# Transposing DMAs on SyncE's queue, low halves at multiples of 16 bytes, and another buffer for the squares, in a four-layer graph kernel

## The chip, the cores and the metric

The kernel runs on one core of one Trainium2 chip. The time is the device time of one execution in microseconds, the median of several runs. The profile is of one further execution.

## The reference

Four graph layers work on x (4096 x 256) and one adjacency matrix adj (4096 x 4096), in float32. Each layer normalises its rows and applies a ReLU, and adds its result to x:

```
def ln_relu(x): return maximum((x - mean(x)) / sqrt(var(x) + 1e-5), 0)     # by rows
h = ln_relu(x);  A2 = adj + I;  s = diagonal(A2) ** -0.5
x = x + relu((s[:, None] * A2 * s[None, :]) @ (A2 @ h @ W0.T))
h = ln_relu(x) @ Wg;  hn = h / maximum(norm(h, rows), 1e-8)
x = x + softmax(hn @ hn.T + log(adj + 1e-8), rows) @ h + bias
h = ln_relu(x);  r = rowsum(adj) ** -0.5
x = x + relu((r[:, None] * adj * r[None, :]) @ h @ W2 + b2)
h = ln_relu(x)
for W in (W3a, W3b): h = relu(concat([h, adj @ h]) @ W)
x = x + h
```

## The kernel before

adj is passed six times (passes 0 to 5 in the code, `p`), each time for one product of the 4096 x 4096 matrix with 256 columns: passes 0 and 1 are the first layer's two products, pass 2 (`ATT`) is attention, pass 3 is the third layer, passes 4 (`TURNED`) and 5 are the last layer. A pass has eight groups `g` of 512 output rows, and a group eight chunks `c` of 512 input rows; a chunk is four blocks of 128. Products run in float16 with every float32 operand split into a high and a low half. The adjacency chunk is split by ScalarE (`ahi`, L771) and VectorE (`alo`, L1035) into one of two buffers; the 256 columns lie in `mov[0]` or `mov[1]` as rows of `MW = 2 * LO` elements per block: the high half, one more column (two are reserved, filled with ones, from F to LO), and the low half from LO on. With `LO = F + 2` the low half begins at byte 516 of a row of 1032 bytes.

TensorE's products per block and 128 output rows: in passes 1, 3 and 5 (`CROSS`) one matmul of 512 columns over both halves (L489) and one of 256 (L490); in passes 0 and 2 three matmuls, of 258 columns (L492), of the 256 of the low half (L493) and of 258 (L494); in pass 4 `mov` is the weights (L500 to L502). The sums of a group are read out by ScalarE (L808, cross terms into `o`) and VectorE (`add_cross`, L1043, which adds into `o`), and only then may TensorE write the bank again (`bank_free`).

A group's results go on during the next group. `PLACES` says after which chunk's split each engine does which step of the group before: "ev" (sums) after chunk 0, "h" (normalised rows, split into `hsp`; VectorE's half is L1149) after 4, "T" after 5, "W0" and "W1" (product of the rows with the layer's weights) after 6, in pass 1 "n0" and "n1" (rows divided by their norm, VectorE's half is L1187) and "G" after 7. `ATT_PLACES` says the same in blocks of attention. TensorE makes the small products of "W0W1" after part 1 of chunk 5 (L582 or L590 first), in attention after block 14 of the first group or 23 of the later ones. They need the rows turned by 128 x 128 blocks: "T" is a transposing DMA from `hsp` to `hT` (`turn_h`, L877), "G" one from `hsp` to `gnT` (`turn_gn`, L883), both issued by ScalarE's queue behind a wait for VectorE's half. There are 24 and 8 of them. ScalarE's groups of passes 1 and 3 are written out; those of passes 0, 4 and 5 are a loop. In pass 1 the squares of a row's values go to `junk` (L903) with their sum beside them; `o` is not in use between the split of the rows and the next group's sums.

SyncE's queue issues all other DMAs. In passes other than attention it is the load of 1 MB of adjacency per chunk (L330) into a ring of four; each waits until the chunk four before has been split (`split_ready`). In attention a step `H` is two blocks: it loads half a chunk (L380) once the numerators up to block 2(H - 3) are there, and, where the exponentials were made in an earlier group (the matrix of cosines is symmetric), a return of them from DRAM (L388), which TensorE turns (L669) three blocks ahead of their use; exponentials for later groups are sent out (L366). ScalarE makes `ahi` of the numerators (L974), VectorE the numerators (L1250) and `alo` (L1257).

```
def load(p, g, c, first=False):
    ...
    sp.wait_ge(split_ready, chunk_no(q, h, e) + 1)
PLACES = {0: ["ev"], 4: ["h"], 5: ["T"], 6: ["W0", "W1"], 7: ["n0", "n1", "G"]}
ATT_PLACES = [{2: ["ev"], 10: ["h"], 11: ["T"], 15: ["W0"], 16: ["W1"], 18: ["n0"], 19: ["n1"], 21: ["G"]},
              {2: ["ev"], 17: ["h"], 18: ["T"], 26: ["W0"], 27: ["W1"]}]
```

Of the kernel before, what the change touches and what calls it, by code (L numbers as in the profile page):

```python
# [41 lines left out]
F = 256  # L42
P = 128
NB = N // P
GB = 4
NG = NB // GB
NC = NB // GB
GR = GB * P
FB = F // P
LO = F + 2  # L50
MW = 2 * LO
LN_EPS = 1e-5
ADJ_EPS = 1e-8
# [3 lines left out]
W_SCALE = 64.0  # L57
# [11 lines left out]
ATT = 2  # L69
TURNED = 4  # L70


def build(nc, x, adj_t, w0, wg, bias_g, w2, bias_2, w3a, w3b, sent, out):
    f32, f16 = mybir.dt.float32, mybir.dt.float16
# [3 lines left out]
    with ctx:  # L78
        def sb(name, shape, dt):
            return ctx.enter_context(nc.sbuf_tensor(name, shape, dt))  # L80
# [4 lines left out]
        def sem(name):  # L85
            return ctx.enter_context(nc.semaphore(name))
# [29 lines left out]
        ev = sb("ev", [P, GB, F + 1], f32)  # L116
        o = sb("o", [P, GB, F], f32)
        oT = o[:, :, :].rearrange("p b n -> p (b n)").rearrange("p (f n) -> p f n", f=FB)
        hsp = sb("hsp", [P, GB, 2, F], f16)

        o2 = nums[:, 0:2, :].rearrange("p b n -> p (b n)").rearrange("p (b n) -> p b n", b=GB)
# [24 lines left out]
        ssq = sb("ssq", [P, GB], f32)  # L146
        ssqc = sb("ssqc", [P, GB], f32)
        rnorm = sb("rnorm", [P, GB], f32)
        junk = sb("junk", [P, GB, F], f16)


        acc = pb("acc", [P, GB, GR], f32)
# [45 lines left out]
        x_ready = sem("x_ready")  # L198
        stats_ready = sem("stats_ready")
        passed = sem("passed")  # L200
        mv_ready = sem("mv_ready")
        var_ready = sem("var_ready")
        rstd_ready = sem("rstd_ready")
# [30 lines left out]
        def at(passes, p, g, per=1, k=1):  # L234
            return (g + NG * passes.index(p)) * per + k
# [78 lines left out]
        def _(sp):  # L314
# [4 lines left out]
            def load(p, g, c, first=False):  # L319
                if not first:  # L320

                    q, h, e = (p, g, c - 4) if c >= 4 else ((p, g - 1, c + 4) if not isinstance(g, int) or g > 0
                                                            else (p - 1, NG - 1, c + 4))
                    if q == ATT:

                        sp.wait_ge(num_ready, h * NB + (GB * (c + 7) if c < 2 else GB * (c + 5)))
                    else:
                        sp.wait_ge(split_ready, chunk_no(q, h, e) + 1)
                row = g * (NC * P) + c * P
                sp.dma_start(ring[c % 4], adj_t[bass.ds(row, P), :]).then_inc(adj_loaded[c % 4], 16)  # L330
# [17 lines left out]
                sp.dma_start(bg[:, :], bias_g[0:1, :].to_broadcast([P, F])).then_inc(b_loaded, 16)  # L348
                sp.dma_start(b2[:, :], bias_2[0:1, :].to_broadcast([P, F])).then_inc(b_loaded, 16)

            def group(p, g, first=False):
                for c in range(2 if first else 0, NC):
                    load(p, g, c, first=first and c < 4)
                    if first and c == 3:
                        load_others()
                    if p == 5 and c == 5 and not isinstance(g, int):
                        store(g - 1)
# [41 lines left out]
            for p in range(6):  # L399
                if p == ATT:  # L400
                    for g in range(NG):
                        for H in range(NH):
                            before = (g, H - 4) if H >= 4 else (g - 1, H - 4 + NH)
                            if before[0] >= 0 and is_sent(*before):
                                send(*before)
                            att_half(g, H)
                else:
                    group(p, 0, first=p == 0)
                    with sp.Fori(1, NG) as g:
                        group(p, g)  # L410
# [68 lines left out]
        def _(pe):  # L479
            def product(p, g, c, b, k, first, last):  # L480


                jb = GB * c + k
                m = mov[p % 2]
                cols = slice(b * P, (b + 1) * P)
                hi, lo = ahi[:, c % 2, k, cols], alo[:, c % 2, k, cols]
                if p in CROSS:
                    both = m[:, jb, :].rearrange("p (s n) -> p s n", s=2)[:, :, 0:F]
                    nc.tensor.matmul(acc[:, b, :].rearrange("p (s n) -> p s n", s=2), hi, both, start=first, stop=False)  # L489
                    return nc.tensor.matmul(acc[:, b, 0:F], lo, m[:, jb, 0:F], start=False, stop=last)  # L490
                n = LO
                nc.tensor.matmul(acc[:, b, 0:n], hi, m[:, jb, 0:n], start=first, stop=False)  # L492
                nc.tensor.matmul(acc[:, b, 0:F], hi, m[:, jb, LO:LO + F], start=False, stop=False)  # L493
                return nc.tensor.matmul(acc[:, b, 0:n], lo, m[:, jb, 0:n], start=False, stop=last)  # L494
# [253 lines left out]
        def _(act):  # L748
# [117 lines left out]
                                     (psT2 if r == 1 else psT)[:, :, :, :].rearrange("p b q n -> p (b q) n"), ACT.Copy)\  # L866
                    .then_inc(hT_kept, 1)

            def turn_h(p, g):

                act.wait_ge(h_ready, at(SMALL, p, g))

                if not isinstance(g, int) or g > 0:
                    act.wait_ge(small_ready, at(SMALL, p, g - 1, 2, 2))
                else:
                    act.wait_ge(small_ready, at(SMALL, SMALL[SMALL.index(p) - 1], NG - 1, 2, 2))
                act.dma_start_transpose(hT[:, :, :], hsp[:, :, :, :].rearrange("p b s n -> p (b s n)"))\  # L877
                    .then_inc(hT_landed, 16)

            def turn_gn(g):  # L880

                act.wait_ge(gn_ready, at([1], 1, g, GB, GB))
                act.dma_start_transpose(gnT[:, bass.ds(g * GB * 2 * FB, GB * 2 * FB), :],  # L883
                                        hsp[:, :, :, :].rearrange("p b s n -> p (b s n)")).then_inc(gnT_landed, 16)

            def small_out(p, b):

                return small_bank(p, b)[:, -F:]

            def hi_of_small(p, g, r):  # L890
                act.wait_ge(small_ready, at(SMALL, p, g, 2, r + 1))
                if p == 3:
                    nc.scalar.activation(directT[:, bass.ds(g * FB, FB), 2 * P * r:2 * P * (r + 1)],
                                         (psW[:, :], psX)[r].rearrange("p (f n) -> p f n", f=FB), ACT.Copy,
                                         scale=1.0 / W_SCALE)\
                        .then_inc(direct_ready, 2)
                for b in (2 * r, 2 * r + 1):
                    if p == TURNED:
                        nc.scalar.activation(direct[:, blocks(g, b), :], small_bank(p, b)[:, 0:F], ACT.Copy, scale=1.0 / W_SCALE)\
                            .then_inc(direct_ready, 1)  # L900
                    if p == 1:

                        nc.scalar.activation(junk[:, b, :], small_out(p, b), ACT.Square, scale=1.0 / W_SCALE,  # L903
                                             accum_out=ssq[:, b:b + 1]).then_inc(ssq_ready, 1)
                    nc.scalar.activation(mov[(p + 1) % 2][:, blocks(g, b), 0:F], small_out(p, b), ACT.Copy,
                                         scale=dinv_w[:, blocks(g, b)] if p == 2 else 1.0 / W_SCALE)\
                        .then_inc(mov_hi, 1)
# [12 lines left out]
            def stage(name, p, g):  # L920

                if name == "ev":
                    evacuate(p, g)
                elif name == "h":
                    if p == 0:
                        hi_of_t(p, g)
                    elif p in SMALL:
                        hi_of_h(p, g)
                elif name == "T":
                    if p in TURN:  # L930
                        turn_h(p, g)
                elif p in SMALL and name in ("W0", "W1"):
                    hi_of_small(p, g, int(name[1]))
                elif p == 1 and name in ("n0", "n1"):
                    hi_of_gn(p, g, int(name[1]))
                elif p == 1 and name == "G":
                    turn_gn(g)


            PLACES = {0: ["ev"], 4: ["h"], 5: ["T"], 6: ["W0", "W1"], 7: ["n0", "n1", "G"]}  # L940
            ATT_PLACES = [{2: ["ev"], 10: ["h"], 11: ["T"], 15: ["W0"], 16: ["W1"], 18: ["n0"], 19: ["n1"], 21: ["G"]},
                          {2: ["ev"], 17: ["h"], 18: ["T"], 26: ["W0"], 27: ["W1"]}]

            def group(p, g, tp, tg):
                for c in range(NC):
# [57 lines left out]
            for p in range(6):  # L1003
                if p == ATT:

                    act.wait_ge(dinv_ready, 2 * NG)
                    for g in range(NG):
                        att_group(g, *((ATT, g - 1) if g else (1, NG - 1)))
                    hi_of_numerators(NG - 1, NB - 1)
                else:  # L1010
                    if p > 0:
                        group(p, 0, p - 1, NG - 1)
                    if p in TURN:

                        for g in range(1, NG):
                            group(p, g, p, g - 1)
                    else:
                        with act.Fori(1, NG) as g:
                            group(p, g, p, g - 1)
            stage("ev", 5, NG - 1)  # L1020


# [337 lines left out]
```

## Time and profile before

| what | value |
|---|---|
| median of 3 runs (lowest to highest) | 2461.54 us (2460.28 to 2462.68) |
| the profiled execution | 2456.39 us |
| its span, first to last instruction | 2454.6 us |
| TensorE busy (PE; weight loads PEld) | 2408.8 us, 98% (1614.4 us, 66%) |
| VectorE (DVE), ScalarE (ACT), GpSimd (POOL) busy | 1450.2, 1082.2, 143.7 us |
| mean granted TensorE clock | 0.996 |
| DMA | 490.00 MB, 200 GB/s |

The profiled execution lies 5.2 us below the median of the runs, 0.2%. Busy is an average over passes with different limits. A matmul's listed duration includes its way through the array, so matmuls that follow each other overlap; their pace is seen in the starts or in counts per time. An engine name with a q (ACTq) is its queue: issuing and waiting, while the engine itself is idle. PEclk or clock is the granted TensorE clock as a share of 2.4 GHz, 0.5 being 1.2 GHz. "DMA to landing" is from issue to the completion.

### The profile page before, as it was taken

Reading aid. Unit: us, or ns where it says so; the run is one execution under the profiler, and the core shown is the slowest. Engines: PE = TensorE matmul, PEld = TensorE weight load, DVE = VectorE, ACT = ScalarE, POOL = GpSimd, SP = SyncE. Lnnn points to the kernel's source line nnn. Section 1 sums busy time; section 2 is a strip of 40 time slices with the busy share of each in tenths; the row PEclk is TensorE's granted clock in tenths of the full one; section 3 lists DMA queues with packets and bytes.
Section 4 is the critical chain, followed back from the end, with each engine's and each line's share of the span. In section 5 each row is a group of like instructions: output and inputs, shape, how many; then the busy total and the mean of one; then the engine's idle time right before and its main releaser. Section 6 shows DMA issues by size and latency. Waiting matters only on the chain.

```text
span 2454.6 us, 41678 instructions
## 1 busy us (share of the span) xinstructions
PE 2408.8 (98%) x16584; PEld 1614.4 (66%) x16584; DVE 1450.2 (59%) x1907; ACT 1082.2 (44%) x1379; POOL 143.7 (6%) x114
## 2 busy tenths in 40 slices
PE   7999999999999999999999999999999999999999
PEld 7888887555556667777888666666544444566665
DVE  7645445675666566666777666566544454455555
ACT  6544444444444444444443444444444334443333
POOL 2300000111111000000000000001000000000000
PEclk9999999999999999999999999999999999999999
DMA  6455555656564866776778656555555445556553
GB/s 241 156 204 192 201 197 198 205 190 201 191 205 137 229 191 200 232 235 211 241 250 249 231 180 199 173 194 198 185 185 184 179 172 187 188 193 216 209 220 137
DMA packets 180289, 490.00 MB, mean 200 GB/s; under 512 B 80993, under 2 KB 114017, under 8 KB 139233
## 3 DMA queue, kind: packets, MB, share of 16 engines
q1 hardware_dynamic: 113344, 471.13, 55.5%
q10 hardware_dynamic: 66848, 17.57, 3.7%
q8 instruction: 63, 1.03, 0.2%
q14 instruction: 34, 0.27, 0.0%
HBM read 438.32 MB, written 33.55 MB: 192 GB/s over the span
## 4 chain that ended last, share of the span: by engine, by line
PE 90%; issue 3%; DVE 2%; ACT 2%; ACTq 1%; POOL 1%; DMA 1%; DVEq 0%; POOLq 0%
PE acc L489 25%; PE acc L490 12%; PE acc L493 8%; PE acc L492 8%; PE acc L494 8%; PE acc L502 5%; PE acc L500 5%; PE acc L501 5%; PE psS L683 2%; PE psS L685 2%; PE psS L684 2%; PE psS L669 2%; ACT ahi L771 1%; POOL rstd L432 1%; DMA hT<-hsp 1%
## 5 line engine op out<-in xcount | busy, mean ns | idle before, releaser
L489 PE MATMUL acc<-mov,ahi 128*128 128x512 f16 x3072 | 1004.2, 380 | 18.2 <-DVE o L1043 17.4
L490 PE MATMUL acc<-mov,alo 128*128 128x256 f16 x3072 | 839.5, 273 | 0.0
L1035 DVE SCALAR_TENSOR_TENSOR alo<-expo,ahi 128x2048 f16<-128x2048 f32 x160 | 366.6, 2291 | 348.4 <-ACT ahi L771 348.4
L492 PE MATMUL acc<-mov,ahi 128*128 128x258 f16 x2048 | 558.4, 273 | 4.8 <-DVE alo L1257 2.9
L493 PE MATMUL acc<-mov,ahi 128*128 128x256 f16 x2048 | 561.1, 274 | 0.0
L494 PE MATMUL acc<-mov,alo 128*128 128x258 f16 x2048 | 556.4, 272 | 0.0
L1035 DVE SCALAR_TENSOR_TENSOR alo<-adj,ahi 128x2048 f16<-128x2048 f32 x160 | 366.6, 2291 | 320.9 <-ACT ahi L771 318.8
L489 PEld LDWEIGHTS acc<-mov,ahi 128*128 128x128 f16 x3072 | 301.3, 98 | 383.6 <-DVE o L1043 19.8
L771 ACT ACTIVATE ahi<-expo 128x2048 f16<-128x2048 f32 x160 | 305.6, 1910 | 479.9 <-PE acc L490 297.5
L771 ACT ACTIVATE ahi<-adj 128x2048 f16<-128x2048 f32 x160 | 305.4, 1909 | 366.4 <-PE acc L490 178.4
L490 PEld LDWEIGHTS acc<-mov,alo 128*128 128x128 f16 x3072 | 301.3, 98 | 35.2
L492 PEld LDWEIGHTS acc<-mov,ahi 128*128 128x128 f16 x2048 | 196.9, 96 | 46.0 <-DVE alo L1257 5.6
L493 PEld LDWEIGHTS acc<-mov,ahi 128*128 128x128 f16 x2048 | 198.0, 97 | 39.5
L494 PEld LDWEIGHTS acc<-mov,alo 128*128 128x128 f16 x2048 | 202.1, 99 | 26.7
L974 ACT ACTIVATE ahi<-nums 128x512 f16<-128x512 f32 x256 | 160.0, 626 | 107.0 <-DVE nums L1250 102.0
L500 PE MATMUL acc<-ahi,mov 128*128 128x512 f16 x512 | 194.0, 379 | 0.0
L501 PE MATMUL acc<-alo,mov 128*128 128x512 f16 x512 | 194.0, 379 | 0.0
L502 PE MATMUL acc<-ahi,mov 128*128 128x512 f16 x512 | 194.0, 379 | 0.0
L1257 DVE SCALAR_TENSOR_TENSOR alo<-nums,ahi 128x512 f16<-128x512 f32 x256 | 175.2, 684 | 5.8 <-ACT ahi L974 5.7
L1250 DVE SCALAR_TENSOR_TENSOR nums<-adj,expo 128x512 f32<-128x512 f32 (+2 forms) x144 | 93.0, 646 | 131.3 <-ACT expo L957 130.8
L957 ACT ACTIVATE expo<-psS 128x512 f32<-128x512 f32 (+2 forms) x144 | 80.9, 562 | 201.9 <-PE psS L685 164.8
L432 POOL TENSOR_TENSOR rstd<-vare,neghalf 128x4 f32<-128x4 f32 x32 | 77.2, 2413 | 1160.2 <-DVE vare L1125 1160.2
(132 smaller groups left out, 2017.4 us busy)
## 6 DMA issues: line engine op xcount, KB each, us to landing
adj<-in_adj_t SPq DMA_DIRECT2D x160, 1024.0 KB, 4.8
expo<-in_adj_t SPq DMA_DIRECT2D x160, 1024.0 KB, 4.8
adj<-in_adj_t SPq DMA_DIRECT2D x128, 512.0 KB, 4.9
sent<-expo SPq DMA_DIRECT2D x112, 256.0 KB, 3.0
expo<-sent SPq DMA_DIRECT2D x56, 512.0 KB, 5.6
xres<-in_x SPq DMA_DIRECT2D x7, 512.0 KB, 10.0
out<-xres SPq DMA_DIRECT2D x7, 512.0 KB, 3.5
xres<-in_x ACTq DMA_DIRECT2D x1, 512.0 KB, 3.5
```

The costliest lines, as they stand in the source:

```text
L489: nc.tensor.matmul(acc[:, b, :].rearrange("p (s n) -> p s n", s=2), hi, both, start=first, stop=False)
L490: return nc.tensor.matmul(acc[:, b, 0:F], lo, m[:, jb, 0:F], start=False, stop=last)
L492: nc.tensor.matmul(acc[:, b, 0:n], hi, m[:, jb, 0:n], start=first, stop=False)
L493: nc.tensor.matmul(acc[:, b, 0:F], hi, m[:, jb, LO:LO + F], start=False, stop=False)
L494: return nc.tensor.matmul(acc[:, b, 0:n], lo, m[:, jb, 0:n], start=False, stop=last)
L500: nc.tensor.matmul(acc[:, f, :], hi, ahi[:, c % 2, k, :], start=first, stop=False)
L501: nc.tensor.matmul(acc[:, f, :], hi, alo[:, c % 2, k, :], start=False, stop=False)
L502: return nc.tensor.matmul(acc[:, f, :], lo, ahi[:, c % 2, k, :], start=False, stop=last)
L771: nc.scalar.activation(ahi[:, c % 2, :, :].rearrange("p b n -> p (b n)"), ring[c % 4], ACT.Copy, scale=ADJ_SCALE)\
L974: nc.scalar.activation(ahi[:, (j // GB) % 2, j % GB, :], nums[:, n % NUMS, :], ACT.Copy, scale=P_SCALE)\
L1035: nc.vector.scalar_tensor_tensor(alo[:, c % 2, :, :].rearrange("p b n -> p (b n)"), ring[c % 4], ADJ_SCALE, ahi[:, c % 2, :, :].rearrange( ...
L1257: nc.vector.scalar_tensor_tensor(alo[:, (j // GB) % 2, j % GB, :], nums[:, n % NUMS, :], P_SCALE, ahi[:, (j // GB) % 2, j % GB, :], ALU.mu ...
```

## The change

Both transposing DMAs move from ScalarE's queue to SyncE's, each behind its waits, which sit on a `sem_inc` of a new semaphore. In passes 1 and 3 the rows' one goes behind the load of chunk 0 and the normalised rows' one behind the load of chunk 3 of the group two later; in attention behind steps given by H. SyncE's first two groups of these passes and the first two of pass 4 are written out, and ScalarE's groups become a loop in every pass but attention. LO becomes F + 8: the low half begins at byte 528, and a row has 1056 bytes. The three-matmul form keeps its 258 columns. The squares go to `o`'s bytes, and `junk` is gone.

```
-LO = F + 2
+LO = F + 8
+        squares = o[:, :, :].rearrange("p b n -> p (b n)").bitcast(f16).rearrange("p (b n) -> p b n", b=2 * GB)
-        junk = sb("junk", [P, GB, F], f16)
+        turning = sem("turning")
@@ SyncE
-            def group(p, g, first=False):
+            def turn_h(p, g):
+                sp.wait_ge(h_ready, at(SMALL, p, g))
+                sp.wait_ge(small_ready, at(SMALL, p, g - 1, 2, 2))
+                sp.sem_inc(turning, 1)
+                sp.dma_start_transpose(hT[:, :, :], hsp[:, :, :, :].rearrange("p b s n -> p (b s n)"))\
+                    .then_inc(hT_landed, 16)
+            def turn_gn(g):
+                sp.wait_ge(gn_ready, at([1], 1, g, GB, GB))
+                sp.sem_inc(turning, 1)
+                sp.dma_start_transpose(gnT[:, bass.ds(g * GB * 2 * FB, GB * 2 * FB), :],
+                                       hsp[:, :, :, :].rearrange("p b s n -> p (b s n)")).then_inc(gnT_landed, 16)
+            def group(p, g, first=False, turned_rows=None):
                 for c in range(2 if first else 0, NC):
                     load(p, g, c, first=first and c < 4)
+                    if turned_rows is not None and c == 0:
+                        turn_h(*turned_rows)
+                    if turned_rows is not None and turned_rows[0] == 1 and c == 3:
+                        turn_gn(turned_rows[1])
...
                             att_half(g, H)
+                            if g == 0 and H == 1:
+                                turn_h(1, NG - 2)
+                            elif g == 0 and H == 3:
+                                turn_gn(NG - 2)
+                            elif g == 0 and H == 8:
+                                turn_h(1, NG - 1)
+                            elif g == 0 and H == 12:
+                                turn_gn(NG - 1)
+                            elif g > 0 and H == 11:
+                                turn_h(ATT, g - 1)
+                elif p in (1, 3):
+                    group(p, 0)
+                    group(p, 1, turned_rows=(ATT, NG - 1) if p == 3 else None)
+                    with sp.Fori(2, NG) as g:
+                        group(p, g, turned_rows=(p, g - 2))
+                elif p == TURNED:
+                    group(p, 0, turned_rows=(3, NG - 2))
+                    group(p, 1, turned_rows=(3, NG - 1))
+                    with sp.Fori(2, NG) as g:
+                        group(p, g)
@@ TensorE
-                n = LO
+                n = F + 2
@@ ScalarE: turn_h and turn_gn, which were there, are gone, and "T" and "G" from stage, PLACES and ATT_PLACES
-                        nc.scalar.activation(junk[:, b, :], small_out(p, b), ACT.Square, scale=1.0 / W_SCALE,
+                        nc.scalar.activation(squares[:, b, :], small_out(p, b), ACT.Square, scale=1.0 / W_SCALE,
-                    if p in TURN:
-                        for g in range(1, NG):
-                            group(p, g, p, g - 1)
-                    else:
-                        with act.Fori(1, NG) as g:
-                            group(p, g, p, g - 1)
+                    with act.Fori(1, NG) as g:
+                        group(p, g, p, g - 1)
```

## Rows read from the trace of the kernel before

**Rows 1.** Windows, passes 0, 4, 5: busy PE, PEld, DVE, ACT, POOL; clock, DMA.

```profile
200.00:380.00 180.00, 180.00 (x1632) 157.88 (x1631) 91.48 (x77) 76.63 (x67) 13.56 (x9) 1.00 0.55 198
...
1800.00:2080.00 280.00, 280.00 (x1299) 126.90 (x1298) 135.48 (x97) 112.61 (x108) 0.00 (x0) 1.00 0.50 180
2180.00:2420.00 240.00, 240.00 (x1479) 144.57 (x1478) 127.59 (x82) 96.24 (x71) 0.00 (x0) 1.00 0.59 212
```

**Rows 2.** Waits of TensorE: total us, times, longest us.

```profile
PE acc L489 <- DVE o L1043: 17.4, 6, 4.3
...
PE acc L492 <- DVE alo L1257: 2.9, 2, 2.2
PE psW L582 <- DMA hT<-hsp: 2.3, 1, 2.3
PE psW L590 <- DMA hT<-hsp: 1.9, 1, 1.9
```

**Rows 3.** Windows of 10 us over gaps in pass 1, attention and pass 3.

```profile
478.00:488.00 10.00, 5.79 (x27) 2.84 (x25) 7.88 (x11) 4.80 (x6) 0.00 (x0) 0.83 0.52 148
525.00:535.00 10.00, 8.40 (x53) 4.89 (x51) 7.21 (x8) 4.91 (x6) 0.00 (x0) 1.00 0.80 243
...
1329.00:1339.00 10.00, 7.83 (x56) 6.43 (x55) 5.07 (x9) 3.04 (x5) 0.00 (x0) 0.83 1.08 234
1435.00:1445.00 10.00, 7.74 (x53) 5.79 (x52) 2.92 (x3) 1.78 (x4) 0.00 (x0) 0.83 0.55 198
```

**Rows 4.** Chain that ended last, 466 to 484 us: start us, us, what.

```profile
473.98 3.95 ACTq L883
...
478.03 1.92 ACT ahi L771
...
482.66 0.39 PE acc L489
```

**Rows 5.** Timeline of VectorE, 470 to 486 us: start us, us, engine, line.

```profile
479.97 2.29 DVE L1035 SCALAR_TENSOR_TENSOR alo<-adj,ahi 128x2048 f16<-128x2048 f32 x1 [6.03 <-ACT ahi L771]
482.18 1.41 DVE L1043 SCALAR_TENSOR_TENSOR o<-acc,o 128x256 f32<-128x256 f32 x4
```

**Rows 6.** Timelines of SyncE, ScalarE and TensorE around 455 to 463 us.

```profile
454.36 5.52 SPq L330 DMA_DIRECT2D adj<-in_adj_t  x2
...
455.32 4.33 ACTq L877 DMA_TRANSPOSE hT<-hsp  x1
...
462.66 0.27 PE L590 MATMUL psW<-wsp,hT 128*128 128x256 f16 x1
```

**Rows 7.** Instructions of line 877: ns shortest/median/longest; DMA to landing.

```profile
L877 ACTq DMA_TRANSPOSE hT<-hsp x24: 1333/4214/4687, 455.3 to 1760.6; - x24
...
DMA to landing us min/median/max: 4.3/6.3/12.1
```

**Rows 8.** The page's DMA issues: times, KB each, median us to landing.

```profile
adj<-in_adj_t SPq DMA_DIRECT2D x160, 1024.0 KB, 4.8
```

**Rows 9.** Chain that ended last, 1325 to 1334 us.

```profile
1327.33 3.81 ACTq L877
```

**Rows 10.** Timelines of SyncE and TensorE in attention; landing of line 388.

```profile
1324.57 0.33 SPq L380 DMA_DIRECT2D adj<-in_adj_t  x1
...
1339.46 0.60 PE L669 MATMUL psS<-ident,expo 128*128 128x128 f32 x4
...
1344.74 0.27 PE L590 MATMUL psW<-wsp,hT 128*128 128x256 f16 x1
...
DMA to landing us min/median/max: 3.3/5.6/10.5
```

**Rows 11.** Timeline of TensorE in pass 0, at 300 us.

```profile
300.00 0.27 PE L492 MATMUL acc<-mov,ahi 128*128 128x258 f16 x1
300.11 0.27 PE L493 MATMUL acc<-mov,ahi 128*128 128x256 f16 x1
300.23 0.27 PE L494 MATMUL acc<-mov,alo 128*128 128x258 f16 x1
```

More of the change, by code:

```diff
@@ L867, in keep_hT @@
                     .then_inc(hT_kept, 1)
[L869 to L874, printed above, removed]
-                else:
[L876 to L884, printed above, removed]
             def small_out(p, b):
@@ L928, in stage @@
                         hi_of_h(p, g)
-                elif name == "T":
-                    if p in TURN:
-                        turn_h(p, g)
                 elif p in SMALL and name in ("W0", "W1"):
@@ L935, in stage @@
                     hi_of_gn(p, g, int(name[1]))
[L936 to L942, printed above, removed]
+            PLACES = {0: ["ev"], 4: ["h"], 6: ["W0", "W1"], 7: ["n0", "n1"]}
+            ATT_PLACES = [{2: ["ev"], 10: ["h"], 15: ["W0"], 16: ["W1"], 18: ["n0"], 19: ["n1"]},
+                          {2: ["ev"], 17: ["h"], 26: ["W0"], 27: ["W1"]}]
             def group(p, g, tp, tg):
@@ L1012, in _ @@
                         group(p, 0, p - 1, NG - 1)
-                    if p in TURN:
-                        for g in range(1, NG):
-                            group(p, g, p, g - 1)
-                    else:
-                        with act.Fori(1, NG) as g:
-                            group(p, g, p, g - 1)
+                    with act.Fori(1, NG) as g:
+                        group(p, g, p, g - 1)
             stage("ev", 5, NG - 1)
```

## The prediction, made before the changed kernel had run

> **What bounds the kernel now.** I read the steady stretches first. In passes 0, 4 and 5 TensorE is busy for the whole of 180, 280 and 240 us [rows 1], so there only the pace of a matmul counts. The other times are in the gaps, so I read next what TensorE waited for [rows 2] and laid stretches of 10 us over the gaps [rows 3]. Six waits of 17.4 us in all end with the sum of a group (L1043). They are borders of groups in pass 1, long and short in turn: three like the one with 5.8 us busy of 10 and three like the one with 8.4 (3 x 4.2 + 3 x 1.6 = 17.4). Behind a long one the granted clock of the 10 us is 0.83: after the standstill TensorE ran some 3.4 us at 1.2 instead of 2.4 GHz, 0.17 of 10 us = 1.7 us of work lost. Short ones have 1.00 and lose nothing more. The reader should see that pass 5, with the same sums, has no gap [rows 1]: what is different in pass 1 is named by the chain of waits [rows 4]. ScalarE's queue issues a transposing DMA (L883) at 473.98 for 3.95 us, and the next ahi (L771) starts behind it at 478.03. The DVE rows [rows 5] follow that: alo at 479.97, sums at 482.18, TensorE at 482.66.
>
> **Part 1, the normalised rows' DMA leaves ScalarE (L883).** What is now late by the issue can start when TensorE ends the sixth chunk. A chunk is 16 pairs of matmuls of 240 us / 740 pairs = 0.324 us, 5.2 us [rows 1]; the group ends at 482.66 - 4.2 = 478.4, so ahi may start at 473.2, while VectorE is busy with those rows until 473.98. Then 473.2 + 1.9 (ahi) = 475.1, + 2.3 (alo) = 477.4, + 0.4 (a quarter of the sums' 1.41) = 477.8 [rows 4, 5]: 0.6 us before TensorE wants the bank. So the gap closes, in the 1.6 us cases too. Gain: 17.4 us, and 3 x 1.7 of the clock = 5.1; 22.5 us. The rolled loop on ScalarE costs some register work at a group's end; pass 5 has it and no gap, so nothing.
>
> **Part 2, where SyncE takes them.** SyncE issues the first load of a group at 454.36 and the next at the end of that row, 5.5 us on [rows 6]; the rows' transposition goes between them, released at 455.32 as now, 4.33 us of issue. It ends at 459.7, 0.1 us after the next load's slot; that load is wanted four chunks (20 us) later. The L883 ones fall likewise behind the load of chunk 3; behind them in SyncE's queue is the load of chunk 4, which only the next group's first split releases. At the start of attention one waits from chunk 5 to chunk 7, and behind it is a half that needs numerators of attention, later still. The `sem_inc` before each carries waits and costs tens of ns. Nothing for these.
>
> **Part 3, when the turned rows land.** They land 4.3 to 12.1 us after issue, median 6.3 [rows 7]. In the typical group issue is at 455.32, so landing at 461.6, and TensorE's small product is due at 462.66 [rows 6]: 1.0 us of slack, in some 14 groups of passes 1 and 3. Two landings are late now, 1.9 us and 2.3 us [rows 2], the second with a clock of 0.83 [rows 3], 1.7 us more. Both have the same work before them as the others, so it is traffic of the other queue, SyncE's next load, that delays them. In one queue that load comes behind. I take both away: 1.9 + 2.3 + 1.7 = 5.9 us. Against it, the transposition now stands behind the load of 1 MB issued 1 us earlier, which lands 4.8 us after issue [rows 8], at 459.2. If the two overlap as now, it lands at 461.6; from the shortest landing (4.3) to the case that it begins only then (459.2 + 4.3 = 463.5, 0.8 us too late), the cost is 0.8 us a group; by the longest landing seen, 12.1, it would be 4.8 us. An earlier landing gains nothing, for TensorE does not wait now. I take 0, the end that the median row is nearest to: 6.3 us is already long against 4.3, as of a transfer that follows the load. The Trainium skill, "DMA: Bandwidth & Descriptors", section "Queues, rings and completion order", says that an engine takes packets of its queues in turn and that the increment lands behind all earlier writes of that engine; that is the same reading of the 12.1, and speaks for one queue.
>
> **Part 4, attention.** Of its gaps 2.9 us in two [rows 2] follow a transposing issue, the longer the one of 3.81 us at 1327.33 [rows 9], with a clock of 0.83 [rows 3]; 4.6 us with the clock. They go. But SyncE waits at step 11 until the rows are split, which is 1327.3, and then issues for 3.8 us: the load that it issued at 1324.57 goes out at 1331.2, and the return of exponentials for block 24 right behind it, at some 1331.6 [rows 10]. Only the last group has such a return there, for a block whose transposition (L669) ran at 1339.46 (three blocks ahead of block 24, and the small product at 1344.74 follows block 23) [rows 10]. Without the 3.9 us of stall it is due at 1335.6. The return lands 3.3, 5.6 or at worst 10.5 us after issue [rows 10]: 1334.9, 1337.2 or 1342.1, so a wait of 0, 1.6 or 6.5 us, the last with 1.7 of clock. Earlier groups' loads have more blocks of time. I take 2.0 (the median, and something for the transposition in front of it): 4.6 - 2.0 = 2.6 us.
>
> **Part 5, the low halves.** In the passes with three matmuls a block (0 and 2) the second one (L493) reads from the low half, which starts at byte 516, 4 past a multiple of 16. 1632 matmuls in 180 us are 544 triples of 330.9 ns for 258 + 256 + 258 columns [rows 1]. One matmul of 512 columns takes 280 us / 1299 = 215.6 ns, and a pair of 512 and 256 takes 324.3 [rows 1]. So 256 columns take 108.7, and the triple should take 326 to 328: there are 3 to 5 ns too many, and the timeline puts them behind L493, 0.12 us to the next start against 0.11 [rows 11]. 2048 triples by 3 ns are 6 us, by 5 ns 10. I take 3.2 ns, 6.5 us, since odd blocks' first matmuls share in it but not all stretches of attention are bound by TensorE. In passes 1, 3 and 5 the low half is the second run of a matmul of 512 and shows nothing (324.3 = 215.6 + 108.7). In pass 4 it is weights, under cover. The Trainium skill, "TensorE: Matmul & The Clock Gate", gives the distance of matmuls by their columns plus a constant, with no word of addresses; by it this part would bring nothing.
>
> **Part 6, the squares' buffer.** The same ScalarE instructions write elsewhere; `o` is free between the split of the rows and the next group's sums, both ordered by waits that are there. The wider memset is at the start: nothing.
>
> Sum: 22.5 + 5.9 + 2.6 + 6.5 = 37.5 us. The profiled execution took 2456.4, so 2418.9; the median of the runs is 5.1 us above it, and I forecast 2461.5 - 37.5 = 2424.0.
>
> **Rivals.**
> (a) The transposition lands 1 to 2.3 us later than now behind the load. Beyond the 1.0 us of slack that is up to 1.3 us in some 14 groups, 18 us, and the two late ones stay (5.9): 37.5 - 5.9 - 18 = 14 us of gain at the worst, 32 at the best, so 2430 to 2448. For it: the shared queue. Against: the typical landing already follows a load.
> (b) The addresses cost nothing, and the 3 ns are of the 258 columns or the weights: 31 us, 2430.5. For it: I know the place of the 3 ns only to 10 ns in the timeline.
> (c) Slower: the same place as (a), but over 3.2 us later. A wait of 2.3 us was followed by the lower clock, one of 1.6 was not [rows 2, 3], so 14 groups would cost 14 x (2.2 + 1.7) = 55 us against the 37.5 - 5.9 = 31.6 that the rest brings: +23 us, 2485. It turns slower where a landing comes some 9.5 us after issue (6.3 + 1.0 of slack + 2.2), for 14 x 2.2 alone is 31. For it: 12.1 us was seen once. Against it: the median, and that nothing new crosses in one queue.
> (d) The moved DMAs free ScalarE, but another wait stands behind them at the border (the load of the next chunk, VectorE's order), and attention's last group stalls by all of 8.2 us: the gain is part 5's alone or less (6.5 - 8.2), so 2455 to 2463.
>
> **How the numbers follow.** Forecast 0.62 (2417 to 2431), (b) 0.12, (a) 0.15, (c) 0.06, (d) 0.05. The measurement tells from no change what is over 0.2%, 5 us. Faster: 0.62 + 0.12 + 0.15 + 0.02 = 0.91; the same 0.03; slower 0.06. The range goes from 2415 (all of part 4's gain, 10 us in part 5, and a little) to 2440, which holds the forecast, (b) and half of (a).
>
> **What would show it.** Right: pass 1 borders busy for 10 of 10 us at clock 1.00; no transposing issue in the chain; no TensorE wait for hT; L493 to L494 0.11 us, and 1650 matmuls in 180 us of pass 0; one gap at most in the last group of attention. Wrong: waits of psW for hT by the dozen (a, c), 1632 matmuls as now (b), or a border gap that ends on a load (d).

## The result, and the profile after

The changed kernel takes 2420.46 us (median of 4 runs, 2419.63 to 2420.89); the kernel before, 2460.91 (4 runs, 2457.95 to 2462.68). The ratio is 0.9836 with an interval of 0.9819 to 0.9853: 1.6% faster, 40.5 us by the medians. The profiled executions are 36.4 us apart (2420.0 against 2456.4).

TensorE's waits of the changed kernel (total us, times, longest us), which answer to [rows 2]:

```profile
PE acc L533 <- DVE o L1057: 1.5, 1, 1.5
PE psS L710 <- DMA expo<-sent: 1.2, 2, 0.8
PE acc L530 <- DVE alo L1049: 0.8, 1, 0.8
```

Lines have moved: L533 to L535 are the former L492 to L494, L530 the former L489, L1049 and L1057 the former L1035 and L1043, L710 the former L669. The six waits of 17.4 us are gone, so are those for hT and the two of attention. The one of 1.5 us is at the start of attention and that of 0.8 us at the start of pass 3; both were there before (1.4 and 0.7). What is new are two waits for returned exponentials.

Windows of the changed kernel, a stretch of pass 0, two borders of pass 1, the last group of attention, and the place in pass 3 where hT was late (span; busy us and count of PE, PEld, DVE, ACT, POOL; clock, DMA share, GB/s):

```profile
200.00:380.00 180.00, 180.00 (x1643) 160.51 (x1642) 91.84 (x77) 76.61 (x66) 14.70 (x9) 1.00 0.55 198
472.00:482.00 10.00, 10.00 (x63) 6.08 (x62) 6.96 (x7) 4.73 (x7) 0.00 (x0) 1.00 0.79 256
516.00:526.00 10.00, 10.00 (x64) 6.00 (x63) 6.91 (x8) 4.73 (x7) 0.00 (x0) 1.00 0.82 256
1298.00:1308.00 10.00, 9.51 (x87) 8.53 (x86) 7.94 (x13) 3.78 (x6) 0.00 (x0) 1.00 0.82 232
1396.00:1406.00 10.00, 10.00 (x70) 6.66 (x69) 4.98 (x3) 3.82 (x2) 0.00 (x0) 1.00 0.89 263
```

Against [rows 3] the borders are busy for 10 of 10 us at full clock. Against [rows 1] pass 0 has 1643 matmuls in 180 us instead of 1632: 328.7 ns for three instead of 330.9.

The timeline of VectorE at the first of these borders shows the working of part 1, instruction by instruction; ScalarE's ahi, which had started at 478.03 [rows 4], ran from 471.34 here, where the group as a whole is some 1.8 us earlier:

```profile
473.29 2.29 DVE L1049 SCALAR_TENSOR_TENSOR alo<-adj,ahi 128x2048 f16<-128x2048 f32 x1 [1.34 <-ACT ahi L812]
475.49 1.08 DVE L1057 SCALAR_TENSOR_TENSOR o<-acc,o 128x256 f32<-128x256 f32 x3
```

And SyncE's queue around it, which answers to [rows 6], shows what took the place of ScalarE's issues:

```profile
452.33 0.34 SPq L331 DMA_DIRECT2D adj<-in_adj_t  x1
453.50 4.30 SPq L357 DMA_TRANSPOSE hT<-hsp  x1
458.07 0.36 SPq L331 DMA_DIRECT2D adj<-in_adj_t  x1
...
472.17 3.60 SPq L364 DMA_TRANSPOSE shared<-hsp  x1
476.06 0.34 SPq L331 DMA_DIRECT2D adj<-in_adj_t  x1
```

The issue is about as long as it was on ScalarE (4.30 and 3.60 us against 4.33 and 3.95). It now stands where nobody waits: the next load goes out right after it.

Where the 36.4 us between the two profiles lie is seen from the first large matmul of each stage in the traces (lengths in us; the middle column is the run of the queue alone, described below):

| stage | before | the queue alone | the change | gained by the change |
|---|---|---|---|---|
| before pass 0 | 22.4 | 22.4 | 22.1 | 0.3 |
| pass 0 | 370.1 | 371.7 | 368.4 | 1.7 |
| pass 1 | 382.5 | 357.4 | 357.4 | 25.0 |
| attention | 588.3 | 586.2 | 583.0 | 5.3 |
| pass 3 | 376.2 | 372.1 | 372.1 | 4.1 |
| passes 4 and 5 | 715.2 | 715.2 | 715.1 | 0.1 |

### The profile page after: what moved, and what is told of

Read it like the earlier page. It is cut to its first block, busy times and chain, and to the rows that moved or that the text cites. A ratio compares the mean times of both kernels' runs of the same rounds, so it can differ in the third digit from the quotient of the medians.

```text
span 2418.2 us, 41920 instructions
## 1 busy us (share of the span) xinstructions
PE 2394.7 (99%) x16584; PEld 1616.3 (67%) x16584; DVE 1452.0 (60%) x1907; ACT 1084.8 (45%) x1379; POOL 147.5 (6%) x114
## 4 chain that ended last, share of the span: by engine, by line
PE 94%; issue 3%; POOL 1%; DMA 1%; DVE 1%; ACT 0%; SPq 0%; POOLq 0%; DVEq 0%; ACTq 0%
PE acc L530 27%; PE acc L531 14%; PE acc L533 8%; PE acc L535 8%; PE acc L534 8%; PE acc L543 5%; PE acc L541 5%; PE acc L542 5%; PE psS L724 2%; PE psS L726 2%; PE psS L725 2%; PE psS L710 2%; POOL rstd L473 1%; PE psS L633 1%; PE psS L631 1%
## 5 line engine op out<-in xcount | busy, mean ns | idle before, releaser
L530 PE MATMUL acc<-mov,ahi 128*128 128x512 f16 x3072 | 999.4, 379 | 0.8 <-DVE alo L1049 0.8
L1049 DVE SCALAR_TENSOR_TENSOR alo<-expo,ahi 128x2048 f16<-128x2048 f32 x160 | 366.7, 2292 | 330.9 <-ACT ahi L812 330.9
L533 PE MATMUL acc<-mov,ahi 128*128 128x258 f16 x2048 | 559.1, 273 | 2.2 <-DVE o L1057 1.5
L535 PE MATMUL acc<-mov,alo 128*128 128x258 f16 x2048 | 559.1, 273 | 0.0
L1049 DVE SCALAR_TENSOR_TENSOR alo<-adj,ahi 128x2048 f16<-128x2048 f32 x160 | 366.8, 2292 | 308.0 <-ACT ahi L812 305.8
L530 PEld LDWEIGHTS acc<-mov,ahi 128*128 128x128 f16 x3072 | 300.6, 98 | 362.2 <-DVE alo L1049 1.1
L533 PEld LDWEIGHTS acc<-mov,ahi 128*128 128x128 f16 x2048 | 200.4, 98 | 37.9 <-DVE alo L1271 2.2
L535 PEld LDWEIGHTS acc<-mov,alo 128*128 128x128 f16 x2048 | 200.4, 98 | 24.9
```

The lines of the kernel that those rows point to most:

```text
L1049: nc.vector.scalar_tensor_tensor(alo[:, c % 2, :, :].rearrange("p b n -> p (b n)"), ring[c % 4], ADJ_SCALE, ahi[:, c % 2, :, :].rearrange( ...
```

## The experiments

All ratios are against the kernel before, run beside each. In a first set it took 2458.53 us (19 runs, 2452.96 to 2466.74), in a second 2459.16 (3 runs), in a third 2458.99 (9 runs).

### The low halves' address alone

```
-LO = F + 2
+LO = F + 8
+        squares = o[...] as float16          # as in the change
-                n = LO
+                n = F + 2
```

> The kernel before with the low halves at byte 528 and the squares in o; the DMAs stay on ScalarE's queue. My theory (the address of the second matmul's columns costs 3 to 4 ns each time): L493 to the next start 109 ns instead of 113, triples some 2.6 to 3.5 ns shorter, 5 to 7 us less than before (2454 to 2456 where before has 2461), and all six border gaps of pass 1 as before, 17.4 us. Rival (the whole gain is of the queues, addresses cost nothing): within 1 us of before.

Measured: 2457.97 us (10 runs, 2449.39 to 2468.43), ratio 0.9995 (0.9976 to 1.0014). The window over pass 0 and the waits of its profile:

```profile
200.00:380.00 180.00, 180.00 (x1643) 160.52 (x1642) 91.92 (x77) 76.61 (x66) 14.70 (x9) 1.00 0.55 198
```

```profile
PE acc L489 <- DVE o L1043: 17.4, 6, 4.2
PE acc L492 <- DVE alo L1257: 3.9, 2, 2.5
...
PE psW L590 <- DMA hT<-hsp: 3.5, 2, 2.5
```

The matmuls run at the changed kernel's pace and the border gaps are all there, as the theory has it. The time does not tell: the executions lie over 19 us, the interval reaches from 5.9 us less to 3.4 us more, and 5 us less is just inside. The next run, held against the changed kernel, shows the step in the time without that scatter.

### The queue alone

```
 the changed kernel, with
-LO = F + 8
+LO = F + 2
```

> The changed kernel with LO = F + 2, that is the DMAs on SyncE's queue and the low halves at byte 516 as before. My theory: no border gap, no wait for the turned rows, L493's successor at 113 ns again; 35 us less than before (2426). With the run of the alignment alone it adds up to the whole change's 40 us. Rival (the parts depend on each other, for instance that the alignment shortens the border): some border gaps stay and the two do not add up by more than 5 us.

Measured: 2427.18 us (4 runs, 2426.40 to 2427.78), ratio 0.9878 (0.9854 to 0.9901): 31 us less than before, and 6.7 us more than the changed kernel. Its windows and waits:

```profile
200.00:380.00 180.00, 180.00 (x1632) 157.87 (x1631) 91.73 (x76) 77.97 (x71) 13.57 (x9) 1.00 0.56 198
```

```profile
PE acc L533 <- DVE o L1057: 1.4, 1, 1.4
PE acc L530 <- DVE alo L1049: 0.7, 1, 0.7
```

No border gap, no wait for hT, and the old pace of 1632. The time is within 1.2 us of the 2426 expected. So the queue's move, together with the squares' buffer and ScalarE's loop, which this kernel has as well, is worth 31 us (24 to 36 by the interval). The step to the changed kernel is the addresses alone, 6.7 us by the medians.

Not all of the 6.7 us can be put down to the addresses. The table of stages above has 3.1 us of it in attention (586.2 against 583.0) and 3.3 in pass 0. Of these 3.3 half is a fall of the clock near the start, which the profile of the queue alone has, that of the changed kernel has not, and a second profile of the same changed kernel (a later run, below) has again. The windows, in that order:

```profile
30.00:40.00 10.00, 7.99 (x64) 6.38 (x64) 6.56 (x20) 5.66 (x13) 1.21 (x2) 0.83 0.75 153
```

```profile
30.00:40.00 10.00, 7.64 (x84) 6.79 (x85) 8.14 (x25) 7.33 (x13) 1.21 (x2) 1.00 0.63 175
```

```profile
30.00:40.00 10.00, 7.99 (x64) 6.34 (x64) 6.57 (x20) 5.67 (x12) 1.21 (x2) 0.83 0.55 162
```

It costs 0.17 of 10 us, 1.7 us, whatever the addresses. Where the clock stayed at 1.00, pass 0 took 370.1 us with byte 516 (before) and 368.4 with byte 528 (the run above and the changed kernel): 1.7 us. So the profiles give the addresses 1.7 + 3.1 = 4.8 us. Attention varies too: in the six profiles with byte 528 and both DMAs on SyncE's queue it took 581.5 to 583.9 us.

### The normalised rows' DMA alone (8 of 32)

```
 the kernel above, with
-                    if turned_rows is not None and c == 0:
-                        turn_h(*turned_rows)
 and without SyncE's turn_h in attention; ScalarE has turn_h and "T" back, its groups are written out again
```

> As the run before this one, but only the normalised rows' transposing DMA (8 of 32) goes to SyncE; the rows' one stays on ScalarE's queue at its old places, and ScalarE's groups stay written out. My theory: the border gaps of pass 1 and their clock go, 22.5 us less than before (2438), and the two late landings (1.9 and 2.3 us, with 1.7 of clock) and the two gaps of attention (0.7 and 2.2, with 1.7) stay. Rival (any transposing issue on ScalarE makes the borders late): gaps at the borders stay, less than 10 us gained.

Measured: 2436.79 us (4 runs, 2431.30 to 2444.00), ratio 0.9926 (0.9898 to 0.9955): 21.7 us less, with an interval of 11 to 25. Its waits:

```profile
PE acc L525 <- DVE alo L1282: 3.3, 2, 2.2
...
PE psS L702 <- DMA expo<-sent: 1.6, 2, 1.0
PE psW L623 <- DMA hT<-hsp: 1.6, 1, 1.6
PE acc L525 <- DVE o L1068: 1.5, 1, 1.5
```

The borders' waits are gone by this move alone. Attention's two gaps (3.3 us) and a late hT stay. Two waits for returned exponentials (1.6 us) are here too, although the rows' DMA has not moved. ScalarE still issues the other 24 without any border being late, so it is this DMA's place, right ahead of the next group's first split, that made them.

### The rows' DMA alone (24 of 32)

```
 the kernel of the queue alone, with
-                    if turned_rows is not None and turned_rows[0] == 1 and c == 3:
-                        turn_gn(turned_rows[1])
 and without SyncE's turn_gn in attention; ScalarE has turn_gn and "G" back, its groups are written out again
```

> The other half: the rows' transposing DMAs (24 of 32) go to SyncE, the normalised rows' one stays on ScalarE's queue. My theory: six border gaps of 17 us with their clock stay, both late landings and attention's two gaps go, two small waits for returned exponentials (0.8 and 0.5 us) come: 9 us less than before (2452). Rival (the late landings come from the load in front, not from the crossing one behind): the waits for hT of 1.9 and 2.3 us stay, 5 us less or nothing.

Measured: 2458.72 us (10 runs, 2457.05 to 2461.94), ratio 1.0007 (0.9994 to 1.0020). Not the 9 us expected, but nothing (by the interval, from 1.5 us less to 4.9 more). The waits say that what should go did go, and that the borders grew:

```profile
PE acc L524 <- DVE o L1064: 22.1, 6, 4.2
...
PE acc L527 <- DVE o L1064: 1.4, 1, 1.4
PE psS L704 <- DMA expo<-sent: 0.8, 2, 0.4
```

No wait for hT, so the rival named in the expectation is out, and none of attention's two gaps, but 22.1 us at the borders instead of 17.4. The windows over the second, third and fourth of its six borders (the other three are like the second, with a clock of 0.83):

```profile
...
527.00:537.00 10.00, 5.78 (x25) 2.86 (x24) 7.36 (x9) 4.80 (x6) 0.00 (x0) 0.83 0.57 159
577.00:587.00 10.00, 5.87 (x23) 2.78 (x22) 7.16 (x8) 4.80 (x6) 0.00 (x0) 0.67 0.58 162
626.00:636.00 10.00, 8.41 (x53) 4.92 (x52) 7.75 (x11) 4.91 (x6) 0.00 (x0) 1.00 0.77 229
...
```

Five are long and one is short, where it was three and three. The clock costs 1.7 + 1.7 + 3.3 + 1.7 + 1.7 = 10.1 us instead of 5.1. So 4.7 us of waits and 5.0 of clock came at the borders, which eats the 9 us. In each trace the short borders are those behind a short issue: the timeline of ScalarE's queue in the kernel before has a long issue for hT and a short one for the normalised rows,

```profile
697.65 4.34 ACTq L877 DMA_TRANSPOSE hT<-hsp  x1
...
716.30 1.33 ACTq L883 DMA_TRANSPOSE shared<-hsp  x1
```

and the lengths of this run's issues in pass 1 (line 907 is `turn_gn` here) are

```profile
L907 ACTq DMA_TRANSPOSE shared<-hsp x6: 1333/3866/3959, 473.9 to 720.9; - x6
```

In the traces of all kernels with transposing DMAs on ScalarE, the fourth of that queue takes 1.33 us, and most of its later multiples of four do as well (in attention and at its end some take up to 2.4 us). In the kernel before both kinds alternated, so every second one of the normalised rows' was a fourth; alone on the queue only every fourth is. That explains one short border in six. Why a fourth issue is short was not tried.

### The rows' DMA one load later

```
-                    if turned_rows is not None and c == 0:
+                    if turned_rows is not None and c == 1:
-                            if g == 0 and H == 1:
+                            if g == 0 and H == 2:
```

> The changed kernel with the rows' transposing DMA one load later in SyncE's queue (behind chunk 1's load in passes 1 and 3, behind step 2's at the start of attention). It measures what the 1.0 us of slack is worth. That load waits for the split of chunk 5, some 4.5 us after the rows are ready. My theory: issue some 4.7 us later, landing 6.2 us after it, so TensorE waits some 3.5 us for hT in 15 or 16 groups, each followed by the lower clock (1.7 us): 80 us more than the changed kernel, 2500, slower than before. Rival (the slack is larger than it looks, because the small product's place gives way): under 1.5 us a group, no fall of the clock, under 25 us more.

Measured: 2530.81 us (2 runs), ratio 1.0289 (1.0255 to 1.0323): 110 us more than the changed kernel, where 80 were expected. Its waits and, in pass 1, its transposing DMA (line 357 in each of these kernels):

```profile
PE psW L623 <- DMA hT<-hsp: 35.1, 8, 4.5
PE psW L631 <- DMA hT<-hsp: 34.6, 8, 4.6
```

```profile
DMA to landing us min/median/max: 7.1/7.1/7.2
```

Sixteen waits, 69.7 us, 4.4 each instead of 3.5, because the landing takes 7.1 us instead of the 6.2 that I had set. Here the DMA is issued some 0.5 us after its load, in the changed kernel 1.2 us after it; that this makes the landing longer was not tried by itself. The clock costs more than I had set, too: in the 10 us around the first of them it is 0.66, not 0.83, and (110 - 69.7) / 16 makes 2.5 us a wait instead of 1.7:

```profile
466.00:476.00 10.00, 8.65 (x45) 5.72 (x46) 1.85 (x6) 3.30 (x13) 2.61 (x3) 0.66 0.34 116
```

That is the case that rival (c) of the prediction describes. The slack is no larger than it looks: a place in SyncE's program one load further on turns the gain of 1.6% into a loss of 2.9%.

### The rows' DMA ahead of the load

```
-                    load(p, g, c, first=first and c < 4)
                     if turned_rows is not None and c == 0:
                         turn_h(*turned_rows)
+                    load(p, g, c, first=first and c < 4)
```

> The changed kernel with the rows' transposing DMA ahead of chunk 0's load instead of behind it. It measures what the load in front costs the landing. My theory (the transposition's packets wait for the load's in the same queue): landing 4.3 to 4.8 us after issue instead of 6.2 in passes 1 and 3, so the slack before TensorE's small product grows from 1.0 to some 2.5 us; the load goes out 5 us later, but it is wanted four chunks later, so the time stays within 1 us of the changed kernel. Rival (the 6.2 us are the transposition's own work): landing at 6 us still.

Measured: 2421.14 us (4 runs), ratio 0.9839 (0.9817 to 0.9861), beside 2420.21 (5 runs) for the changed kernel. Line 357 in pass 1, this run's two rows first, then the changed kernel's:

```profile
L357 SPq DMA_TRANSPOSE hT<-hsp x7: 1783/2007/4382, 455.2 to 720.4; - x7
DMA to landing us min/median/max: 4.3/4.3/6.5
```

```profile
L357 SPq DMA_TRANSPOSE hT<-hsp x7: 4098/4247/4354, 453.5 to 718.7; - x7
DMA to landing us min/median/max: 5.8/6.1/6.4
```

The load in front costs the landing 1.8 us and the issue 2.2 us. Without it both are short, as the expectation had it (4.3 to 4.8 us). (The seventh, 6.5 us, is at the start of attention, where its place was not changed.) The time does not change, as TensorE did not wait for it. The issue of 4 us on ScalarE, with the load in the other queue, had the same length, which suggests that the load counts in whichever queue it is; no run took it away there. What exactly the issue waits for isn't shown: two of the fourth ones of `hT` on ScalarE's queue in pass 3 of the kernel before took 1.33 us with the same load in front.

### Attention's rows one step later

```
-                            elif g > 0 and H == 11:
+                            elif g > 0 and H == 12:
```

> The changed kernel with attention's rows turned behind step 12 instead of step 11 of a group. My theory (SyncE's wait for the rows and its issue hold back step 12's load and return): the two waits of L710 for returned exponentials (0.75 and 0.49 us) go or shrink, the rest stays: 1 us less, which the times cannot tell and the waits can. Rival (the returns are late because DMAs are full in the last groups): both waits stay within 0.3 us, or others come in their place.

Measured: 2418.61 us (2 runs), and no wait for exponentials at all in its profile. As this was the one version that could beat the changed kernel, both ran again side by side in five rounds:

> The changed kernel once more, as the reference for the two runs beside it: 2420.5, two waits of L710 for returned exponentials.

> The kernel with attention's rows turned behind step 12 once more, in more rounds, as a version that may beat the changed kernel: no wait of L710, 1.2 to 2 us less than the changed kernel run beside it (2418.6 against 2420.5). Rival: within 0.5 us of it, the two waits being made up elsewhere.

Measured: 2420.21 us (2419.51 to 2421.71) for the changed kernel and 2420.28 (2418.57 to 2420.90) for the later step; ratios 0.9836 (0.9818 to 0.9855) and 0.9833 (0.9815 to 0.9852). In this profile of the later step the wait of the last group is gone, and two others are in earlier groups:

```profile
PE psS L710 <- DMA expo<-sent: 1.0, 1, 1.0
PE psS L710 <- DVE nums L1264: 0.8, 1, 0.8
```

The wait of the last group, 0.35 to 0.50 us, is in all eight profiles with `turn_h` behind step 11 and in neither of the two with step 12: SyncE's blocking accounts for that. The other waits come and go between executions, and the run of the normalised rows' DMA alone had two of them without this blocking. It is not a faster version that these runs can show.

### Other addresses

```
-LO = F + 8
+LO = F + 4        # and, in another run, F + 6
```

> The changed kernel with LO = F + 4: the low halves at byte 520, 8 past a multiple of 16, rows of 1040 bytes. Theory A (any start off a multiple of 16 costs): the second matmul's successor at 111 to 113 ns. Theory B (only starts off a multiple of 8 cost, in before 4 and 12 past): 109 ns, and the time of the changed kernel within 1 us. The kernel before speaks a little for a small cost of 8 (its first matmuls of odd blocks started 8 past and took 0.7 ns more).

> The changed kernel with LO = F + 6: the low halves at byte 524, rows of 1048 bytes, so even blocks read the low half from 12 past a multiple of 16 and odd ones from 4 past (1048 + 524), as in the kernel before. Theory A and B both: the second matmul's successor at 112 to 113 ns as in before, 5 us more than the changed kernel (2425). Rival (it was the 516 bytes or a reach over the row, not the start): 109 ns.

Measured: 2423.65 us for F + 4 and 2422.85 for F + 6 (2 runs each; ratios 0.9853 and 0.9850). The windows over the same 180 us of pass 0, F + 4 first, then F + 6:

```profile
200.00:380.00 180.00, 180.00 (x1634) 157.87 (x1632) 91.65 (x77) 76.62 (x66) 13.59 (x9) 1.00 0.56 198
```

```profile
200.00:380.00 180.00, 180.00 (x1638) 158.17 (x1636) 92.08 (x77) 76.62 (x66) 13.81 (x9) 1.00 0.55 198
```

The last column but one of the table is the mean time, in the same stretch, from the start of the second matmul (the one that reads the low half) to the next start.

| low half begins at | rows of | three matmuls in pass 0 (180 us / count x 3) | second matmul to the next start | time |
|---|---|---|---|---|
| byte 516 (the queue alone) | 1032 bytes | 330.9 ns | 112.6 ns | 2427.2 us |
| byte 520 | 1040 bytes | 330.5 ns | 112.7 ns | 2423.7 us |
| byte 524 | 1048 bytes | 329.7 ns | 110.2 ns | 2422.9 us |
| byte 528 (the change) | 1056 bytes | 328.7 ns | 109.2 ns | 2420.5 us |

Theory A holds in its direction: every version with starts off a multiple of 16 is slower than the one with none, 8 bytes off included, so "a multiple of 8 will do" falls. That F + 6 would be as slow as before was wrong: it lies half-way. Yet its low halves lie 12 and 4 bytes past a multiple of 16 in turn, the same two remainders as with byte 516 (4 and 12). In pass 0 with byte 516 the second matmul is slow in every block (112.9 and 112.3 ns); with byte 524 it is slow in even blocks (112.1) and not in odd ones (108.3), whose third is slow instead (111.9). So the remainder alone does not set the cost, and what does stays open. The times differ by more than the pace makes (3.5 us between byte 516 and 520, where 0.4 ns for 2048 triples is under 1 us): the fall of the clock at 30 us, 1.7 us, which the profile with byte 516 has and those with 520 and 524 have not, is part of that in the profiles.

## Why the prediction was right

The forecast was 2424.0 us, the range 2415 to 2440; measured 2420.5. Step by step:

- Part 1 (22.5 us): right. The waits (17.4 us) and their clock (5.1) are gone in the profile after, and moving that DMA alone gave 21.7 us (11 to 25). Pass 1 as a whole is 25.0 us shorter, where parts 1 and 3 have 22.5 + 1.9 = 24.4 in it. The sums began at 475.49; the working had 477.4, in a group 1.8 us later.
- Part 2 (nothing): right. The issues stand between the loads, and no wait for a load appeared.
- Part 3 (5.9 us, slack kept): right in what it says of the time. No wait for hT is left, landings in pass 1 are 5.8 to 6.4 us, and pass 3 is 4.1 us shorter, where this part has 2.3 + 1.7 = 4.0 in it. Wherever these DMAs stayed on ScalarE's queue, a late one was in the profile (one of 1.6 us, two of 3.5 together); at the change's place in SyncE's queue there was none in any profile. That it was SyncE's next load, crossing them in another queue, that made the late ones late is argued and was not tried. That the typical landing already follows the load is shown: with the load in front gone it lands 1.8 us sooner.
- Part 4 (2.6 us): the mechanism right, the terms mis-sized. The two gaps (2.9 us and 1.7 of clock) went. Against them the working set 2.0 us for a late return in the last group, and it was 0.5, since SyncE's issue took 1.70 us there and not 3.8, with no 1 MB load just in front of it:

```profile
1298.67 1.70 SPq L357 DMA_TRANSPOSE hT<-hsp  x1
```

  The other wait (0.75 us, in an earlier group) I had excluded; such waits also come with the DMA on ScalarE's queue. So the waits alone would make 4.1 us. The length of attention with byte 516 fell by 2.1 us only (588.3 to 586.2), and in the run of the normalised rows' DMA alone, with the rows' DMA at its old place, it was 590.8. Between executions it moves by as much as this part is worth, so that 2.6 came close is in part luck.
- Part 5 (6.5 us): the mechanism right, the term too large by the profiles. Rival (b) is out: the pair that differs in nothing else is 6.7 us apart, the pace rose, and the second matmul's next start came 109.2 ns after it instead of 112.6, as said. But the working set 3.2 ns for a triple and it was 2.2, so 1643 matmuls in 180 us and not 1650: the triple with all starts on a multiple of 16 takes 328.7 ns (329.2 by the starts) and not 326 to 328, because each of the two matmuls of 258 columns takes 110.0 ns there and 109.2 or 109.6 beside the slow one. The profiles give 4.8 us in all; that the medians came out at 6.7, nearer the term, can be the clock at the start, and is then luck. The Trainium skill, "TensorE: Matmul & The Clock Gate", section "Back-to-back issue gap", gives columns / 2.4 + 2.5 ns as the gap of matmuls by themselves, weight loads left out; by it an estimate is 109.2 ns for 256 columns and 110.0 for 258. With byte 528 the trace agrees (109.2, 110.0 and 110.0), and with byte 516 it does not (112.6 for the 256 columns of the low half). So that rule, which rival (b) followed, does not hold for every address here.
- Part 6: right so far as it shows. Every kernel but the one before has the squares in `o`, so their move was not run by itself.

The stages of the two profiles account for the whole 36.4 us: 0.3 before pass 0, 1.7 in pass 0, 25.0 in pass 1, 5.3 in attention and 4.1 in pass 3, against 37.5 forecast. The medians are 40.5 apart against the first runs of the kernel before and 38.5 against its later ones: the kernel before varies by 14 us from execution to execution, so no sum can be checked closer against it. The nearness of 2424.0 to 2420.5 rests in part on this.

## What to carry to other kernels

An engine's queue that also issues DMAs stops the engine for the length of the issue (here 3.95 us at a long border); look for issue entries in the chain that ended last, and ask whether a queue that only waits for loads has room between two of them. Before placing the issue there, compare the slack of who uses it with one load's distance, for one load too late cost 110 us here. Where two matmuls of the same number of columns differ by a few ns from start to start, compare the addresses at which their moving columns begin.

## What the runs showed of the hardware that I had not expected

- In passes 1 and 3 the issue of the rows' transposing DMA takes 1.7 to 2.1 us with no 1 MB load just before it and some 4.2 with one, on SyncE's queue; on ScalarE's, with the load in SyncE's, it took 4.2 too. On ScalarE's queue the fourth takes 1.33 us, and with it the gaps of quite another place change.
- Taking a cause away can lengthen another: the rows' DMAs alone moved for nothing, the normalised rows' for 21.7 us, both for 31 us. 31.3 - 21.7 = 9.6 us is what the first move is worth once the second is made (3.5 to 17.6 by the single executions; ScalarE's loop, which came with it, is in this too).
- The scatter of the time goes with the place of the rows' DMA: with it on ScalarE's queue the executions spread over 14 us (before), 19 us and 13 us; with it on SyncE's over 4.9, 1.4 and 2.2 us (the run of the rows' DMA alone, that of the queue alone, and the changed kernel, all nine runs). Late landings that differ from one execution to the next would do that; it was seen in one profile each and not tried by itself.
